# Layer 1 of a four-layer graph stack: W2's dot products, low parts and scores in other blocks, and row loads between the halves of turned adj

## What is computed

```python
# layer 0: graph convolution
d = sum(adj.T, axis=1) ** -0.5
y = (d[:, None] * adj.T * d[None, :]) @ (h @ W0) + bias
# layer 1: incidence
head = (adj > 0); head = head / sqrt(sum(head * head, axis=-1))
inc = adj + head
y = (inc @ h) / sum(inc, axis=-1)
# layer 2: attention, 4 heads of 256
ht = (h @ W2) by head
src, dst = ht . a_src, ht . a_dst
att = softmax(leaky_relu(src[:, None] + dst[None, :], 0.01) + adj)
y = mean over heads of att @ ht
# layer 3: binary weights
y = relu(adj @ (max(sign(h), 0) @ sign(W3).T))
```

## Time and profile before

| what | us |
|---|---|
| median of three executions | 732.15 (730.83 to 732.44) |
| the profiled execution | 727.12 |
| its span, first to last instruction | 724.8 |
| TensorE busy in the span | 691.0 (95%) |
| VectorE busy | 629.4 (87%) |
| ScalarE busy | 472.4 (65%) |
| GpSimd busy | 135.6 (19%) |
| layer 1 on TensorE, block 2 to block 15 | 168.97 to 274.1 |

### The profile page before, as it was taken

One profiled execution on the slowest core, in us unless ns is written; L12 is line 12 of the kernel. 1 busy time (PEld: TensorE's weight loads), 2 busy tenths in 40 slices (PEclk: granted clock), 3 DMA queues, 4 the chain that ended last, 5 costly groups with the idle time before them and its releaser, 6 DMA issues.

```text
span 724.8 us, 16131 instructions
## 1 busy us (share of the span) xinstructions
PE 691.0 (95%) x6480; PEld 586.1 (81%) x6480; DVE 629.4 (87%) x1161; ACT 472.4 (65%) x814; POOL 135.6 (19%) x162
## 2 busy tenths in 40 slices
PE   3998999986999999999999999999999999999998
PEld 3676888875888885468888888888888888888887
DVE  6898579688999854799999999989999899998683
ACT  3887153648887624886557867578766778667660
POOL 3962721301223220001210021200121000000000
PEclk9999999998999999999999999999999999999999
DMA  9997999677499887759988779997999831126791
GB/s 337 342 318 238 426 424 309 201 185 219 134 275 277 190 175 234 162 127 243 235 193 235 176 166 257 199 267 161 229 224 228 267 129 30 30 81 188 255 392 46
DMA packets 146457, 159.54 MB, mean 220 GB/s; under 512 B 90896, under 2 KB 103888, under 8 KB 141904
## 3 DMA queue, kind: packets, MB, share of 16 engines
q1 hardware_dynamic: 127328, 117.10, 53.7%
q0 software_dynamic: 19056, 41.42, 25.4%
HBM read 76.15 MB, written 52.46 MB: 177 GB/s over the span
## 4 chain that ended last, share of the span: by engine, by line
PE 60%; DVE 21%; ACT 6%; DMA 4%; issue 4%; SPq 2%; POOL 2%; ACTq 0%; DVEq 0%; POOLq 0%
PE ps L835 11%; PE ps L837 11%; PE ps L836 11%; DVE arena L1473 6%; PE ps L775 6%; DVE arena L1480 5%; PE ps L877 4%; PE ps L878 4%; DVE arena L1346 2%; DMA arena<-in_adj_dram 2%; SPq L383 2%; ACT arena L1003 2%; PE ps L719 2%; PE ps L721 1%; PE ps L720 1%
## 5 line engine op out<-in xcount | busy, mean ns | idle before, releaser
L835 PE MATMUL ps<-arena 128*128 128x257 f16 x1024 | 279.9, 273 | 1.0 <-DVE arena L1480 0.6
L837 PE MATMUL ps<-arena 128*128 128x257 f16 x1024 | 279.4, 273 | 0.0
L836 PE MATMUL ps<-arena 128*128 128x257 f16 x1024 | 279.2, 273 | 0.0
L1168 ACT ACTIVATE arena<-arena 128x512 f16<-128x512 f32 x252 | 158.3, 628 | 93.8 <-PE ps L837 56.3
L1473 DVE SCALAR_TENSOR_TENSOR arena<-arena,w_j 128x512 f32<-128x512 f32 x256 | 190.2, 744 | 0.0
L1480 DVE TENSOR_TENSOR arena<-arena 128x512 f16<-128x512 f32 x256 | 175.7, 687 | 8.1 <-ACT arena L1168 7.8
L835 PEld LDWEIGHTS ps<-arena 128*128 128x128 f16 x1024 | 99.9, 98 | 15.0 <-issue 1.4
L836 PEld LDWEIGHTS ps<-arena 128*128 128x128 f16 x1024 | 100.3, 98 | 12.5
L837 PEld LDWEIGHTS ps<-arena 128*128 128x128 f16 x1024 | 99.8, 97 | 12.9
L719 PE MATMUL ps<-arena 128*128 128x257 f16 x256 | 71.1, 278 | 1.9 <-DVE arena L1298 1.9
L721 PE MATMUL ps<-arena 128*128 128x257 f16 x256 | 70.5, 275 | 0.0
(11 more groups left out here) (154 smaller groups left out, 1154.9 us busy)
## 6 DMA issues: line engine op xcount, KB each, us to landing
adj_t<-arena POOLq DMA_DIRECT2D x32, 1024.0 KB, 7.9
arena<-in_adj_dram SPq DMA_DIRECT2D x32, 512.0 KB, 6.0
arena<-in_adj_dram SPq DMA_DIRECT2D x16, 1024.0 KB, 5.8
adj_parts<-arena SPq DMA_DIRECT2D x16, 1024.0 KB, 25.7
arena<-adj_t SPq DMA_DIRECT2D x64, 256.0 KB, 4.5
arena<-adj_t SPq DMA_DIRECT2D x16, 1024.0 KB, 6.7
x<-arena POOLq DMA_DIRECT2D x15, 512.0 KB, 5.7
arena<-u_rows SPq DMA_DIRECT2D x4, 1024.0 KB, 14.7
```

What stands on the lines that cost most here:

```text
L835: mm(ps[:, bank, 0:DE], hi, ht_hi[:, head, j, 0:DE], start=s, stop=False)
L836: mm(ps[:, bank, 0:DE], hi, ht_lo[:, head, j, 0:DE], start=False, stop=False)
L837: ins = mm(ps[:, bank, 0:DE], lo, ht_hi[:, head, j, 0:DE], start=False, stop=e)
L1168: nc.scalar.activation(p_hi[:, j % 4, :], prob[:, j % 4, :], copy).then_inc(p_hi_done, 1)
```

## The change

Four things move, and no arithmetic is added or left out.

- VectorE: the sixteen dot products go from blocks 1 to 4 to blocks 12 and 13, eight each. The split of `wa` goes from block 5 to block 14. The quarters of W2's low part go from blocks 5 to 8 to blocks 14 and 15, two each. The maximum goes from block 12 to block 11. The buffer for the products that nobody reads has eight slots in place of four.
- TensorE: scores 0 to 13 all stand behind block 15's products, in place of five behind block 6 and one behind each of the blocks 7 to 15.
- SP: `turn_adj` issues one half at a time, and rows 12, 13, 14 and 15 are loaded each behind one of the four halves of `turn_adj(0)` and `turn_adj(1)`. Every row load waits for a `fill` as before.

```diff
--- before.py
+++ after.py
@@ -154,7 +154,7 @@
         h2_lo = view(85 * KB, [2, D], F16)
         h2_relu = view(86 * KB, [2, D], F32)
         w2_f = view(72 * KB, [DC, HD], F32)
-        wa_junk = view(80 * KB, [4, D], F32)
+        wa_junk = [view((80 + 57 * (k // 4) + k % 4) * KB, [D], F32) for k in range(2 * HEADS)]
         h2_t = view(H2T, [2 * DC, N], F16)
         w2_hi = view(H2T + 16 * KB, [DC, HD], F16)
         w2_lo = view(H2T + 20 * KB, [DC, HD], F16)
@@ -374,15 +374,14 @@
                     sp.dma_start_transpose(out=inc_parts[t % AHEAD][:, part, :, :], in_=inc_nat[t % 2][:, part, :]
                                            ).then_inc(inc_in[t % AHEAD], 16)
 
-            def turn_adj(n):
+            def turn_adj(n, part):
                 q, g = n // TG, n % TG
-                if n >= 2:
+                if n >= 2 and part == 0:
                     sp.wait_ge(wide[(n - 2) % TG], 16 * ((n - 2) // TG + 1))
                 slot = (turn_l1 if q == 0 else turn_l2)[n % 2]
-                for part in range(2):
-                    sp.dma_start_transpose(out=slot[:, part, :, :],
-                                           in_=nat_dram[TG * P * g:TG * P * (g + 1), part, QB * P * q:QB * P * (q + 1)]
-                                           ).then_inc(turned[n % 2], 16)
+                sp.dma_start_transpose(out=slot[:, part, :, :],
+                                       in_=nat_dram[TG * P * g:TG * P * (g + 1), part, QB * P * q:QB * P * (q + 1)]
+                                       ).then_inc(turned[n % 2], 16)
 
             sp.wait_ge(nat_lo_done, HALVES)
             for t in range(2):
@@ -420,11 +419,12 @@
                 sp.wait_ge(nat_sent[k], 16 * (SENT[k][1] - SENT[k][0]))
             for n in range(2):
                 sp.wait_ge(inc_in[4 - n], 32)
-                turn_adj(n)
-            for t in range(12, NB):
-                reload_rows(t)
+                for part in range(2):
+                    turn_adj(n, part)
+                    reload_rows(12 + 2 * n + part)
             for n in range(2, QB):
-                turn_adj(n)
+                for part in range(2):
+                    turn_adj(n, part)
 
 
             def load_e(q):
@@ -452,7 +452,8 @@
             sp.wait_ge(ht_ps, 2 * NB)
             for q in range(1, NQ):
                 for g in range(TG):
-                    turn_adj(QB * q + g)
+                    for part in range(2):
+                        turn_adj(QB * q + g, part)
                 load_e(q)
             for i in range(2):
                 sp.dma_start(adjt_early[i], adjt_dram[i]).then_inc(adjt_in[4 + i], 16)
@@ -757,12 +758,10 @@
                     products1(t, g)
                     if g == 1 and t >= 2:
                         h2_transposes(t - 2)
-                    if g == 3 and t == 6:
+                    if g == 3 and t == 15:
                         pe.wait_ge(wa_done, 1)
-                        for k in range(4):
+                        for k in range(NB - 2):
                             scores(k)
-                    if g == 3 and t >= 6:
-                        scores(t - 2)
 
             def ht_block(t, halves=(0, 1)):
                 for half in halves:
@@ -1327,7 +1326,7 @@
                 for h in heads:
                     for side in range(2):
                         k = side * HEADS + h
-                        v.tensor_tensor_reduce(wa_junk[:, 2 * (h % 2) + side, :], w2_f[:, c, h * D:(h + 1) * D],
+                        v.tensor_tensor_reduce(wa_junk[2 * h + side], w2_f[:, c, h * D:(h + 1) * D],
                                                a_bc[:, (2 * h + side) * D:(2 * h + side + 1) * D],
                                                W_SCALE, 0.0, ALU.mult, ALU.add, wa[:, c, k:k + 1]
                                                ).then_inc(wa_part, 1)
@@ -1423,19 +1422,20 @@
                     part_low(t + 3, 3)
                 if t >= 1:
                     h2_low(t - 1)
-                if 1 <= t <= 4:
-                    if t == 1:
-                        dve.wait_ge(w2_in, 32)
-                    w2_a((t - 1) // 2, (2 * ((t - 1) % 2), 2 * ((t - 1) % 2) + 1))
-                if t == 5:
+                if t == 12:
+                    dve.wait_ge(w2_in, 32)
+                if t in (12, 13):
+                    w2_a(t - 12, range(HEADS))
+                if t == 14:
                     w2_a_parts()
                     dve.wait_ge(w2_hi_done, 1)
-                if 5 <= t <= 8:
-                    c, half = (t - 5) // 2, (t - 5) % 2 * 512
-                    v.scalar_tensor_tensor(w2_lo[:, c, half:half + 512], w2_f[:, c, half:half + 512], W_SCALE,
-                                           w2_hi[:, c, half:half + 512], ALU.mult, ALU.subtract
-                                           ).then_inc(w2_lo_done, 1)
-                if t == 12:
+                if t in (14, 15):
+                    for half in range(0, 1024, 512):
+                        c = t - 14
+                        v.scalar_tensor_tensor(w2_lo[:, c, half:half + 512], w2_f[:, c, half:half + 512], W_SCALE,
+                                               w2_hi[:, c, half:half + 512], ALU.mult, ALU.subtract
+                                               ).then_inc(w2_lo_done, 1)
+                if t == 11:
                     dve.wait_ge(max_made, NB + 1)
                     v.tensor_reduce(amax[:, 0:1], nat_max, AX_X, ALU.max).then_inc(amax_part, 1)
             row_sums(NB - 1)
```

## The result

The change made the kernel 0.46% slower: the ratio of the times is 1.0046, 95% interval [1.0027, 1.0066]. Over 20 runs each, the medians are 732.04 us after (729.39 to 738.24) and 729.38 us before (725.47 to 733.15), a difference of 2.7 us. The three runs of before that stand ahead of the prediction were thus on the slow side of their own kernel. In all that follows one single run is left out as a slow one: the twelfth of f3, 806.88 us at a mean granted clock of 0.852.

The account below looks back on a forecast made before the run. TensorE was taken to bound layer 1, with 2.95 us idle to win. Stall 4.75 plus VectorE's end 0.3 less 2.95 gave +2.1 us on a median of 732.15: 734.2 us, range 730.4 to 738.0.

Parts of the forecast that it names:

- The bound: Layer 1: it ends when TensorE is through its list; its 2.95 us of idle time is the most to win.
- The gain of 1.36 us: TensorE's waits of 0.52, 0.55 and 0.29 us go, through lighter VectorE blocks and an earlier row 12.
- The issue of the half: SP's queue: the second half of turn 1, behind row 14 and `fill(11)`, goes out at 216.5 us.
- Its landing: The second half of turn 1 takes 7.8 us and lands at 224.3 us.
- GpSimd's stall: GpSimd reaches `widen_high(1)` at about 219.4 us and stands there until 224.3.
- The chain to TensorE: From GpSimd's wait to TensorE 10.75 us; TensorE goes on with block 10 at 235.05, idle 4.75 us.
- The second stall: At `inverse_root2(8)`: none, as `widen_high(1)` lands in 6.4 us, under the 6.6 limit; the 1.59 us wait goes.
- case B: Rival: both stalls, `widen_high(1)` needing 10.3 us, 3.7 us more, 737.9 us; chance 0.12 together with Case D.
- The end of layer 1 on VectorE: Moved VectorE work delays the last `w2_lo` before `h2_transposes(14)` by 0.3 to 1.3 us; 0.3 taken.
- the scores: TensorE: fourteen scores only move, behind block 15, at no price; TensorE reaches block 10 1.3 us earlier.
- Case D: Rival: TensorE's waiting halves the clock, costing 3.3 us more, 737.5 us; chance 0.12 together with case B.
- the forecast's own case: Late half stalls GpSimd and TensorE: +2.1 to +4.0 us, down to +0.5 with a shorter landing; chance 0.52.

Follow-up runs that it names:

- f3: Kernel before with only SP's new load order, plus `widen_high(1)` and `add_low(1)` a block later on GpSimd; ratio 0.9958, median 725.63 us.
- e3: Changed kernel with `widen_high(1)` and `add_low(1)` a block later on GpSimd; ratio 0.994, median 725.29 us.
- f2: Kernel before with only `widen_high(1)` and `add_low(1)` a block later on GpSimd; ratio 1.0009, median 729.68 us.
- f5: Changed kernel with GpSimd's steps on all four slots spread over blocks 6 to 14; ratio 0.9907, median 722.11 us.
- f7: Kernel before with GpSimd's steps spread over blocks 6 to 14 as in f5; ratio 0.9922, median 724.81 us.
- f9: The kernel of f2 profiled a second time, nothing else changed; that execution took 728.31 us.
- e1: Kernel before with SP's part of the change alone, a row load behind each turned half; ratio 1.0039, median 732.14 us.
- e2: Changed kernel with SP's old order, both slots turned, then rows 12 to 15; ratio 1.0013, median 729.64 us.
- f1: Changed kernel with 72 unread matmuls ahead of `h2_transposes(7)` to keep the clock up; ratio 1.0033, median 731.84 us.
- f8: Kernel before, unchanged, profiled a second time; 729.52 us, one run.
- f6: f5 with 110 unread matmuls on TensorE ahead of block 2; ratio 0.9881, median 721.81 us.
- e4: Changed kernel with only row 12 loaded between the two turned slots, rows 13 to 15 behind both; ratio 1.0014, median 729.53 us.

## Why the prediction was right, step by step

**The bound** held. Less TensorE's waits, layer 1 is 107.5 (e3) to 108.8 us (before) long in all seven profiles without added matmuls in which the clock did not fall after 174 us (before, e3, f2, f3, f5, f7, f9). But the waits are not worth their sum: in before, after, e1, e2, f1 and f8 the last one ends with GpSimd's chain, and what is won ahead of it counts only as far as it moves that chain too.

**The gain of 1.36 us** came: none of the waits of 0.52, 0.55 and 0.29 us is left in after, while e1, without VectorE's part, keeps the first two. That their going shortens layer 1 shows in f5 beside f7 (2.02 us) and in e3 beside f3 (1.42 us), but not in e2.

**The issue of the half** was put at 216.5 and came at 215.20, since `fill(11)` ended at 212.46 + 2.34 = 214.80 and not 215.9. 1.3 us to the good.

**Its landing** was the term mis-sized: 7.8 us taken, 11.2 measured, beyond the 9.7 that was meant to bound it. The choice was made by the order on SP's own queue. The four landings of after speak for the other reading, by what GpSimd has under way. The halves of 193.59 and 200.67 have a row load ahead and no transfer of GpSimd's under way, and take 7.8 and 6.4; those of 207.94 and 215.20 have `widen_high(0)` (issued at 209.96) and `add_low(0)` (219.74) beside them, and take 11.7 and 11.2. f5 varies this: it issues `add_low(0)` at 223.61, when the half of 214.32 has landed, and that half took this long:

```profile
DMA to landing us min/median/max: 8.0/8.0/8.0
```

It took 8.2 us in f6, but 10.1 to 11.2 in the five kernels with `add_low(0)` beside it (after, e1, e3, f1, f3). So 2 to 3 of the missing 3.4 us are `add_low(0)`'s, and 7.8 was the figure for a half without it. That each DMA engine takes packets from its queues in turn, as the Trainium skill says (DMA: Bandwidth & Descriptors, section Queues, rings and completion order), agrees with this in direction. The estimate of 2.0 us that the same page's 261 GB/s gives for the bytes, section Latency and other measured facts, was met by no half here; the nearest took 4.1.

**GpSimd's stall** of 4.9 us was 5.54, for two errors that cancel. The half landed 2.1 us later than forecast, and GpSimd came later too, at 221.1 instead of 219.4, because `add_low(0)` stood 2.46 us for `widen_high(0)`. That wait was not foreseen: before, `widen_high(0)` was issued at 212.5 and landed in 6.4 us; in after it goes out at 209.96, beside the late half, and needs 9.5.

**The chain to TensorE** was 10.75 us by the text and 236.82 - 226.66 = 10.16 in after, 10.15 in e1. TensorE's idle time by it was 4.75 us and is 4.43 + 0.15 = 4.58, with 2 us of slowed matmuls between the two, so that it goes on with row 13 at 236.82 and not at 235.05. It stands nearly whole in block 9; the text put it in block 10, with "some of it already in block 9".

**The second stall** was said to be away and is half there. GpSimd went on 7.2 us behind the issue of `widen_high(1)` (233.86 - 226.66) where 6.6 was the limit (the landing itself took 6.9, near the 6.4 taken), and `inverse_root2(8)` took 2.46 us directly behind `add_low(1)`. 1.67 us of waiting is left at 245.97 where the forecast had struck out 1.59. That is the sign of case B with less than half of its 3.7 us.

**The end of layer 1 on VectorE** and the scores cost nothing: no wait stands before `h2_transposes(14)`, and the 0.69 us at the last score is there in every kernel. The 0.3 us should have been 0, the lower end of what was given.

**Case D** happened together with the forecast's own case: the text had it as a rival and argued that the pieces of the wait would not bring the clock down. In after it is one piece of 4.43 us, and the clock fell: for 6.8 us in after and e4, for 3.4 in e1, e2 and f8. Its price of 3.3 us was wrong for this place. The slower matmuls took 2 us of after that TensorE would have waited anyway, and f1 puts the cost at nothing; in e4, where no such wait follows, it is 2.8.

The measured time lies in the range, and the sign is the one given most weight. That +2.1 us comes so near to the 2.7 between the medians is in part luck. Against the profile from which the sum was made, layer 1 grew by 5.35 us: 3.98 at the first transposes of row 13, where the sum has 235.05 - 232.98 = 2.07; 0.04 off in the second stall, where it takes 1.59 off; 1.41 for the moved scores, where it has 1.3; and nothing at VectorE's end, where it has 0.3. The idle time alone, +3.3 us, hides 2 of these behind the slower matmuls. The medians differ by less, and f8 suggests why: an execution of before can have most of such a stall already. That 734.2 lies above the measured 732.04 is owed to the base, not to the sum: the three runs shown of before had a median of 732.15, and twenty have 729.38, to which the same sum would have given 731.5.

**What stays open.** Why `inverse_root2(8)` takes 1.09 us behind `add_low(1)` in before and 1.3 to 2.8 in after, e1, e2 and f1, in after most of the second stall. Why `widen_high(1)` takes 10.3 us in one execution of before and 13.5 in another; no run varied that alone. The loss per execution can't be read more closely than that spread, since f8 and the first profile of before differ by 3.26 us in layer 1.

## What to carry to other kernels

A step that waits for a transfer should not share an in-order engine with small steps that others wait for: here a 0.6 us `inverse_root2` behind a wait for a landing held TensorE up for 4.6 us, against the 1.36 us of waits that VectorE's part removed. Follow the waits to the last one before the end: an earlier wait that is won counts only as far as it brings the last one forward (e2), and a slower clock cost nothing ahead of that one (f1) and 2.8 us behind it (e4). When a queue is reordered so that an early load comes earlier, follow the one that is now last to its consumer, and ask when that consumer comes for it; moving the consumer by a block under the new queue (e3) or spreading its steps (f5, f7) was worth 0.6 to 0.9% where reordering the queue alone lost 0.4%. And profile the kernel before twice: its own waits can differ between executions by as much as the change is worth.

## What the runs showed of the hardware

- A turned half took 4.1 to 11.7 us to land in layer 1, for the same bytes; those of 10 us and more all had a transfer of GpSimd's beside them. The same half took 8.0 and 8.2 us without `add_low(0)` beside it (f5, f6) and 10.1 to 11.2 with it.
- The granted clock fell to 0.50 around TensorE waits of 2.34 (e2), 2.88 (e4), 2.96 (f8), 3.19 (e1) and 4.43 us (after). In e3, f9 and f1 waits of 1.63, 1.76 and 2.04 us left it at 1.00. In before it took 6.63 us of idling to see it, so I had thought it a matter of long waits.
- `inverse_root2`, one value per partition, took 0.59 us alone, 1.09 us behind `add_low(1)` in before, and 2.46 us in the same place in after, 2.75 in e2; spans on GpSimd are rough, but ScalarE's start at 237.28 confirms the 2.46.
